# Norms applied on GpSimd to the residual's columns, their statistics spread through DRAM

## The chip, the cores and the metric

The kernel runs on one core of one Trainium2 chip. The metric is the device time of one execution in microseconds (us).

## What is computed

The input is X with 16 x 256 = 4096 tokens of width 128, float32. The block is an FFN, an attention and the FFN again, each added to the residual x:

```python
x = x + 0.5 * ffn(layernorm(x))
x = x + attn(layernorm(x))
x = x + 0.5 * ffn(layernorm(x))
# ffn (hidden width 512, ternary weights w, column scales s; lin(x, w, s) = (x @ w.T) * s)
h = silu(lin(x, w1, s1)) * lin(x, w2, s2)
h = gelu(lin(h, h1, sh1))
h = gelu(lin(h, h2, sh2))
return lin(h, w3, s3)
# attn
h = layer_norm(x) * gamma + beta
keys, values = h @ Wk.T + bk, h @ Wv.T + bv
w = exp((keys @ Wka.T + bka) / sqrt(128))
w = w / cumsum(w, over a sequence of 256)
return cumsum(w * keys) * values
```

## The kernel before

**Tiles.** The 4096 tokens are eight tiles of 512. The residual lies transposed in SBUF as `xt_sb`, with the 128 features on the partitions and the tokens as columns. A second copy of the input, `x_sb`, has tokens on the partitions in blocks of 128. Each tile goes through FFN step t (t = 0 to 7), attention step t (0 to 7), and FFN step t + 8.

**An FFN step.** `p1.m` multiplies the normalised tile with w1 and w2 (m = 0 to 3 are the four blocks of 128 hidden units), ScalarE takes `tanh`, VectorE forms `gate` and `up`. `p2.m`, `gelu2.m` are the second layer, `p3.m`, `gelu3.m` the third, `p4` the last; `dt` adds its result to the residual. TensorE multiplies float32r numbers, so each activation is split: ScalarE's `high` copies it rounded, VectorE's `low` (`act_lo`) subtracts that copy from the full value, and every product is two matmuls. A chunk of p2 or p3 is eight matmuls of 128x128 with 128x512, a chunk of p1 four, p4 eight.

**A norm** (24 of them: 8 for each of the three parts). `stats` is bn_stats on VectorE over blocks with tokens on the partitions. For the first FFN they are blocks of `x_sb`; for attention and the second FFN TensorE first transposes the residual's tile into the PSUM bank `y_ps` (stage `u`, four 128x128 transposes). `aggr` and `veps` on VectorE make mean and variance, `norm` on GpSimd makes `rstd` with a power and `nmr` = -mean x rstd. ScalarE writes the normalised blocks to `z` (`z`, four activations of 128x128), TensorE transposes them into `xt_ps` (stage `t`, four transposes), ScalarE copies that to `xn_hi` and VectorE forms `xn_lo` (FFN), or ScalarE applies gamma and beta and writes `h_t` (attention).

**An attention step.** Three float32 matmuls of `h_t`: `logits` (keys' and logits' weights are folded), `keys`, `values`. ScalarE writes `kw` (exp) and `keys`. VectorE runs `cumsum`, `recip.0`, `recip.1`, `weight` (kw x 1/cumsum), `weight_keys` (x keys), `pool` (cumsum again), `values` and `dt`, which adds to the residual.

**What sets the order.** Every engine works its queue in order; the queues are written out by hand in strings (`START`, `FIRST_STEP`, `ORDER`, `LAST_STEP`), one item per stage and chunk. A step is one FFN tile's second to fourth layer, with the next tile's p1 and the norm after that mixed in (`AHEAD` says how many tiles ahead an item works). The attention items `a:` and `b:` stand in a pattern of three steps that is repeated. Waits are semaphores inside the stages. SyncE's queue loads everything first and then stores the finished tiles. Three flags say whether the weights are exact in float32r; with the given inputs the fast branch runs.

Of the kernel before, what the change touches and what calls it, by code (L numbers as in the profile page):

```python
# [89 lines left out]
LAST_STEP = {  # L90
    "PE": "p2.0 p2.1 p2.2 p2.3 p4 p3.0 p3.1 p3.2 last:p4a last:p3.0 last:p3.1 last:p4b last:p4c.0 last:p4c.1",
    "ACT": "gelu2.0 gelu2.1 high2.0 high2.1 gelu2.2 high2.2 gelu2.3 high2.3 gelu3.0 high3.0 gelu3.1 high3.1 "
           "gelu3.2 high3.2 last:gelu.0 last:gelu.1",
# [905 lines left out]
```

## Time and profile before

| what | value |
| --- | --- |
| median of 3 runs | 377.42 us (376.82 to 377.8) |
| profiled execution, span from first to last instruction | 374.9 us |
| between that span and the median of the runs | 2.5 us |
| PE busy | 368.0 us, 98% |
| DVE (VectorE) busy | 321.9 us, 86% |
| ACT (ScalarE) busy | 314.1 us, 84% |
| POOL (GpSimd) busy | 52.6 us, 14% |

No device time is listed for the profiled execution itself, so its span is set against the median of the other runs. Busy is the time in which an engine has an instruction of its own running; matmuls are pipelined, so their records overlap and their starts, not their durations, tell what one costs.

### The profile page before, as it was taken

Reading aid. Unit: us, or ns where it says so; the run is one execution under the profiler, and the core shown is the slowest. Engines: PE = TensorE matmul, PEld = TensorE weight load, DVE = VectorE, ACT = ScalarE, POOL = GpSimd, SP = SyncE. Lnnn points to the kernel's source line nnn. Section 1 sums busy time; section 2 is a strip of 40 time slices with the busy share of each in tenths; the row PEclk is TensorE's granted clock in tenths of the full one; section 3 lists DMA queues with packets and bytes.
Section 4 is the critical chain, followed back from the end, with each engine's and each line's share of the span. In section 5 each row is a group of like instructions: output and inputs, shape, how many; then the busy total and the mean of one; then the engine's idle time right before and its main releaser. Section 6 shows DMA issues by size and latency. Waiting matters only on the chain.

```text
span 374.9 us, 5278 instructions
## 1 busy us (share of the span) xinstructions
PE 368.0 (98%) x1662; PEld 291.9 (78%) x1662; DVE 321.9 (86%) x713; ACT 314.1 (84%) x549; POOL 52.6 (14%) x67
## 2 busy tenths in 40 slices
PE   7999999999999999999999999999999999999996
PEld 2678888787787877778788787778877778788885
DVE  5898787999999799999988999989799999976733
ACT  4999699989977999798699979967998998686763
POOL 3531101202101202201021120102101210020000
PEclk9999999999999999999999999999999999999999
DMA  7760000000000000000000000000000000000001
GB/s 246 277 265 1 2 0 0 1 2 1 0 2 0 1 2 2 2 0 1 2 0 1 2 1 28 2 28 1 2 29 0 0 30 1 30 1 28 2 0 58
DMA packets 4494, 9.81 MB, mean 26 GB/s; under 512 B 625, under 2 KB 1905, under 8 KB 4209
## 3 DMA queue, kind: packets, MB, share of 16 engines
q1 hardware_dynamic: 3744, 8.65, 6.3%
q10 hardware_dynamic: 720, 0.80, 0.6%
q8 instruction: 15, 0.25, 0.2%
q14 instruction: 15, 0.11, 0.1%
HBM read 7.35 MB, written 2.10 MB: 25 GB/s over the span
## 4 chain that ended last, share of the span: by engine, by line
PE 95%; DMA 2%; DVE 1%; SPq 1%; issue 0%; ACT 0%; ACTq 0%
PE hid_ps L449 60%; PE gate_ps L449 8%; PE y_ps L449 7%; PE up_ps L449 7%; PE xt_ps L462 3%; DMA x_sb<-x 2%; PE y_ps L462 2%; PE xt_ps L632 2%; PE xt_ps L629 2%; PE xt_ps L635 2%; PE up_ps L507 1%; PE gate_ps L507 1%; DVE gate L855 0%; PE xt_ps L449 0%; DVE xt_sb L924 0%
## 5 line engine op out<-in xcount | busy, mean ns | idle before, releaser
L449 PE MATMUL hid_ps<-act_hi,hi_h 128*128 128x512 f32 x480 | 195.6, 408 | 0.0
L449 PE MATMUL hid_ps<-act_lo,hi_h 128*128 128x512 f32 x480 | 186.8, 389 | 0.0
L877 DVE TENSOR_TENSOR act_lo<-full,act_hi 128x512 fp32r<-128x512 f32 x185 | 122.2, 683 | 26.8 <-ACT act_hi L708 24.3
L701 ACT ACTIVATE full<-hid_ps,vec 128x512 f32<-128x512 f32 x123 | 84.4, 686 | 34.9 <-PE hid_ps L449 31.2
L449 PEld LDWEIGHTS hid_ps<-act_hi,hi_h 128*128 128x128 f32 x480 | 90.1, 188 | 22.4 <-issue 4.1
L449 PEld LDWEIGHTS hid_ps<-act_lo,hi_h 128*128 128x128 f32 x480 | 90.2, 188 | 22.1 <-issue 4.3
L708 ACT ACTIVATE act_hi<-full 128x512 fp32r<-128x512 f32 x127 | 78.5, 630 | 2.3
L362 POOL TENSOR_TENSOR rstd<-veps,half 128x4 f32<-128x4 f32 x24 | 35.2, 1467 | 272.5 <-DVE veps L840 272.5
L855 DVE SCALAR_TENSOR_TENSOR gate<-tanh,gate_ps 128x512 f32<-128x512 f32 x60 | 40.6, 679 | 9.2 <-ACT tanh L684 8.6
L684 ACT ACTIVATE tanh<-gate_ps,s_half 128x512 f32<-128x512 f32 x60 | 40.8, 686 | 8.2 <-PE gate_ps L449 8.2
L867 DVE SCALAR_TENSOR_TENSOR full<-up_ps,s_half,gate 128x512 f32<-128x512 f32 x60 | 44.2, 742 | 0.9
L689 ACT ACTIVATE act_hi<-full 128x512 fp32r<-128x512 f32 x60 | 37.3, 621 | 0.2
L940 DVE RECIPROCAL rcsum<-csum 128x256 f32<-128x256 f32 x16 | 27.9, 1743 | 0.0
L449 PE MATMUL gate_ps<-xn_hi,hi_w 128*128 128x512 f32 x59 | 24.7, 419 | 0.0
L726 ACT ACTIVATE z<-y_ps,nmr,rstd 128x128 f32<-128x128 f32 x64 | 24.0, 460 | 0.8 <-POOL nmr L364 0.8
L449 PE MATMUL y_ps<-act_hi,hi_w 128*128 128x512 f32 x60 | 24.2, 403 | 0.0
L449 PE MATMUL y_ps<-act_lo,hi_w 128*128 128x512 f32 x60 | 23.5, 392 | 0.0
L449 PE MATMUL gate_ps<-xn_lo,hi_w 128*128 128x512 f32 x59 | 23.0, 390 | 0.0
L449 PE MATMUL up_ps<-xn_lo,hi_w 128*128 128x512 f32 x59 | 23.0, 390 | 0.0
L449 PE MATMUL up_ps<-xn_hi,hi_w 128*128 128x512 f32 x59 | 23.0, 390 | 0.0
L825 DVE BATCH_NORM_STATS2 stats<-y_ps 128x6 f32<-128x128 f32 x64 | 14.2, 285 | 0.0
L462 PE MATMUL xt_ps<-ident,z 128*128 128x128 f32 x90 | 13.6, 273 | 0.0
(159 smaller groups left out, 397.8 us busy)
## 6 DMA issues: line engine op xcount, KB each, us to landing
xt_sb<-xt SPq DMA_DIRECT2D x1, 2048.0 KB, 10.9
out<-xt_sb SPq DMA_DIRECT2D x7, 256.0 KB, 2.0
x_sb<-x SPq DMA_DIRECT2D x1, 1536.0 KB, 6.6
raw_h<-h2t SPq DMA_DIRECT2D x4, 256.0 KB, 7.3
raw_h<-h1t SPq DMA_DIRECT2D x2, 256.0 KB, 5.9
raw_w<-w2t ACTq DMA_DIRECT2D x1, 256.0 KB, 4.0
raw_w<-w1t SPq DMA_DIRECT2D x1, 256.0 KB, 3.8
raw_h<-h1t ACTq DMA_DIRECT2D x1, 256.0 KB, 6.7
```

The lines of the kernel that those rows point to most:

```text
L362: eng.tensor_tensor(rstd[:, :], veps[:, :], half[:, :], ALU.pow).then_inc(s_pow, 1)
L449: mm = eng.matmul(ps, w, a, start=(first and n == 0), stop=(last and n == len(seq_) - 1))
L462: mm = eng.transpose(dst[:, j * P:(j + 1) * P], src[:, j * P:(j + 1) * P], ident[:, :])
L684: eng.activation(tanh_b[m % 2][:, :], gate_home(T, m)[:, :], ACT.Tanh, scale=s1_half[:, m:m + 1]).then_inc(s_tanh, 1)
L689: eng.activation(act_hi[first_act(T)][:, m, :], full1[m % 2][:, :], ACT.Copy).then_inc(s_hi[1], 1)
L701: eng.activation(full23[m % 2][:, :], home23(n, T, m)[:, :], ACT.Gelu, scale=col("sh1" if n == 2 else "sh2", m)).then_inc(s_gelu[n], 1)
L708: eng.activation(act_hi[n][:, m, :], full23[m % 2][:, :], ACT.Copy).then_inc(s_hi[n], 1)
L726: zz = eng.activation(z[:, j * P:(j + 1) * P], norm_blk(kind, t, j), ACT.Identity, bias=nmr[:, j:j + 1], scale=rstd[:, j:j + 1])
L855: eng.scalar_tensor_tensor(gate_b[m % 2][:, :], tanh_b[m % 2][:, :], 1.0, gate_home(T, m)[:, :], ALU.add, ALU.mult).then_inc(s_gate, 1)
L867: eng.scalar_tensor_tensor(full1[m % 2][:, :], up_home(T, m)[:, :], s12_half[:, m:m + 1], gate_b[m % 2][:, :], ALU.mult, ALU.mult).then_in ...
L877: eng.tensor_tensor(act_lo[a][:, m, :], full[m % 2][:, :], act_hi[a][:, m, :].bitcast(F32), ALU.subtract).then_inc(s_lo[n], 1)
L940: eng.reciprocal(rcsum[:, b], csum[:, b]).then_inc(s_rc, 1)
```

## The change

The first three norms (FFN tiles 0, 1 and 2) stay as they are. The other 21 are made another way:

- VectorE makes only `stats`, now into one of two buffers. `aggregate` on GpSimd combines the two halves of each bn_stats record in seven short operations and takes the power; it leaves -mean and 1/std of all 512 tokens in `pair_b`, 128 partitions x 2 x 4.
- `spread` on SyncE writes these 1024 numbers to a row in DRAM in token order (`rows`), waits until they have landed, and loads the row (4 KB) into every one of the 128 partitions of `wide_b`.
- `xn.0` and `xn.1` on GpSimd add -mean to the residual's tile `xt_tile(t)` and multiply by 1/std, 128x512 each, into `xnt_b`. ScalarE's `t` and VectorE's `t` read `xnt_b` in place of `xt_ps`. The activations to `z` and the transposes `t` are gone.
- The bank `y_ps` is free again after `stats`, not after z.
- In attention `weight` is now kw x keys and `weight_keys` multiplies that by 1/cumsum; the operations are of the same form and number on VectorE.
- The repeated pattern is replaced by sixteen orders for each engine, one per step (`STEPS`), with SyncE's and GpSimd's among them. Items are named by their tile (`a5:stats`, `12:u`); the stores stand among the spreads.

The core of the diff (the other steps' orders, semaphores and the two-buffer bookkeeping are left out). Of the orders, those of steps 7 to 14 of PE, 11 and 12 of ScalarE, and 11 to 13 of VectorE are shown:

```diff
+    "SP": (
...
+        "spread 10:store 11:store store",
+        "store",
+        "store",
+    ),
+    "POOL": (
...
+        "a5:norm a5:xn.0 a5:xn.1 norm 12:norm xn.0 xn.1",
+        "xn.0 xn.1",
+        "a6:norm a6:xn.0 a6:xn.1 norm xn.0 xn.1",
+        "a7:norm a7:xn.0 a7:xn.1 norm xn.0 xn.1",
+        "norm xn.0 xn.1",
...
+        "a3:logits p1.0 p1.1 p2.0 p4 a3:keys u p2.1 p2.2 p2.3 p1.2 a4:u p3.0 p1.3 p3.1 10:u p3.2 p3.3",
+        "a3:values p1.0 p1.1 p2.0 p2.1 p2.2 p2.3 p4 p1.2 p1.3 a4:logits a5:u p3.0 p3.1 a4:keys p3.2",
+        "p1.0 8:p3.3 a4:values p1.1 p4 p2.0 u p2.1 p2.2 p2.3 p1.2 a5:logits 12:u p1.3 p3.0 p3.1 a5:keys p3.2 "
+        "p3.3",
+        "p1.0 p1.1 p2.0 p2.1 p4 p2.2 p2.3 a5:values a6:u p1.2 p1.3 p3.0 p3.1 p3.2 p3.3",
+        "p1.0 p1.1 p2.0 p4 p2.1 u p2.2 p2.3 a7:u p1.2 a6:logits p1.3 p3.0 p3.1 a6:keys p3.2 a6:values p3.3",
+        "p1.0 p1.1 p2.0 p2.1 p4 p2.2 u p2.3 a7:logits p1.2 p1.3 p3.0 p3.1 a7:keys p3.2 a7:values p3.3",
+        "p1.0 p1.1 p2.0 p4 p2.1 u p2.2 p2.3 p1.2 p1.3 p3.0 p3.1 p3.2 p3.3",
+        "p2.0 p2.1 p1.0 p4 p1.1 p2.2 p2.3 p1.2 p1.3 p3.0 p3.1 p3.2 p3.3",
...
+        "tanh.1 gelu2.0 gelu2.1 high2.0 a6:t high2.1 gelu2.2 high2.2 gelu2.3 high1.0 high1.1 tanh.2 high2.3 "
+        "a6:logits tanh.3 gelu3.0 high3.0 a6:keys high1.2 gelu3.1 13:t high1.3 high3.1 gelu3.2 gelu3.3 "
+        "high3.2 high3.3",
+        "gelu2.0 high2.0 tanh.0 tanh.1 gelu2.1 high2.1 gelu2.2 a7:t high2.2 gelu2.3 high1.0 high2.3 tanh.2 "
+        "high1.1 tanh.3 a7:logits high1.2 gelu3.0 a7:keys high3.0 high1.3 gelu3.1 14:t high3.1 gelu3.2 "
+        "high3.2 gelu3.3 high3.3",
...
+        "gate.0 a5:dt dt up.0 stats gate.1 low2.0 up.1 low2.1 low2.2 a7:stats low1.0 gate.2 low2.3 low1.1 "
+        "up.2 a6:cumsum a6:recip.0 gate.3 a6:recip.1 up.3 13:t low3.0 low1.2 low3.1 low1.3 a6:weight "
+        "a6:weight_keys low3.2 a6:pool low3.3",
+        "low2.0 a6:values gate.0 a6:dt dt gate.1 stats low2.1 up.0 low2.2 up.1 low1.0 low2.3 gate.2 up.2 "
+        "gate.3 low1.1 a7:cumsum up.3 low1.2 a7:recip.0 a7:recip.1 low3.0 14:t low3.1 a7:weight low1.3 "
+        "a7:weight_keys low3.2 a7:pool low3.3",
+        "a7:values a7:dt dt gate.0 stats low2.0 low2.1 up.0 gate.1 up.1 low2.2 low1.0 low2.3 low1.1 gate.2 "
+        "up.2 gate.3 low3.0 up.3 low1.2 low3.1 low1.3 low3.2",
...
+BY_PE = (0, 1, 2)
+AGGREGATE = 3
...
+        wide_b = [sb(f"wide_{i}", [P, 2 * TOK]) for i in range(2)]
+        xnt_b = [sb(f"xnt_{i}", [P, TOK]) for i in range(2)]
+        rows = nc.dram_tensor("rows", [2, 2 * TOK], F32).ap()
...
+            def spread(kind, t):
+                i, use = slot(kind, t)
+                eng.wait_ge(s_pow, norm_of[kind, t] + 1)
+                if use > 0:
+                    eng.wait_ge(s_wide[i], 16 * use)
+                eng.dma_start(rows[i].rearrange("(q j p) -> p q j", q=2, j=SUB), pair_b[i][:, :, :],
+                              allow_slow_non_contiguous=True).then_inc(s_parked[i], 16)
+                if use > 0:
+                    eng.wait_ge(s_xn, wide_of[kind, t] - 1)
+                eng.wait_ge(s_parked[i], 16 * (use + 1))
...
+                eng.dma_start(wide_b[i][:, :], rows[i].partition_broadcast(P)).then_inc(s_wide[i], 16)
...
+            def aggregate(n, kind, t):
+                i, use = slot(kind, t)
+                stats, done = stats_b[n % 2], 6 * (n - AGGREGATE)
+                a, b = (1.0 + EPS, EPS * EPS) if n in att_norms else (1.0, EPS)
+                eng.wait_ge(s_bn, SUB * n + SUB)
+                if use > 0:
+                    eng.wait_ge(s_parked[i], 16 * use)
+                eng.tensor_tensor(pair_diff[:, :], stats[:, :, 1], stats[:, :, 4], ALU.subtract).then_inc(s_agg, 1)
+                eng.tensor_tensor(pair_sum[:, :, :], stats[:, :, 1:3], stats[:, :, 4:6], ALU.add).then_inc(s_agg, 1)
+                eng.wait_ge(s_agg, done + 1)
+                eng.tensor_tensor(diff_sq[:, :], pair_diff[:, :], pair_diff[:, :], ALU.mult).then_inc(s_agg, 1)
+                eng.wait_ge(s_agg, done + 2)
+                eng.tensor_scalar(var_part[:, :], pair_sum[:, :, 1], a / P, b, ALU.mult, ALU.add).then_inc(s_agg, 1)
+                eng.wait_ge(s_agg, done + 3)
+                eng.tensor_scalar(diff_part[:, :], diff_sq[:, :], a / 4.0, None, ALU.mult).then_inc(s_agg, 1)
+                eng.tensor_scalar(pair_b[i][:, 0, :], pair_sum[:, :, 0], -0.5, None, ALU.mult).then_inc(s_agg, 1)
+                eng.wait_ge(s_agg, done + 5)
+                eng.tensor_tensor(veps[:, :], var_part[:, :], diff_part[:, :], ALU.add).then_inc(s_ve, 1)
+                eng.wait_ge(s_agg, done + 6)
+                eng.wait_ge(s_ve, n + 1)
+                eng.tensor_tensor(pair_b[i][:, 1, :], veps[:, :], half[:, :], ALU.pow).then_inc(s_pow, 1)
+
+            def xn_add(kind, t):
+                i, use = slot(kind, t)
+                eng.wait_ge(s_wide[i], 16 * (use + 1))
+                if use > 0:
+                    before, at = by_wide[wide_of[kind, t] - 2]
+                    eng.wait_ge(*((s_xlo, at) if before == "ffn" else (s_ht, at + 1)))
+                if kind == "att":
+                    eng.wait_ge(s_x1, t + 1)
+                elif t < NT:
+                    eng.wait_ge(s_xt, 16)
+                else:
+                    eng.wait_ge(s_x2, t - NT + 1)
+                eng.tensor_tensor(xnt_b[i][:, :], xt_tile(t), wide_b[i][:, 0:TOK], ALU.add).then_inc(s_centred, 1)
+
+            def xn_mult(kind, t):
+                i, _ = slot(kind, t)
+                eng.wait_ge(s_centred, wide_of[kind, t] + 1)
+                eng.tensor_tensor(xnt_b[i][:, :], xnt_b[i][:, :], wide_b[i][:, TOK:2 * TOK], ALU.mult).then_inc(s_xn, 1)
...
-            for n in range(2, 3 * NT):
-                norm(n)
...
-                    elif stage == "u" and t >= NT:
+                    elif stage == "u":
                         eng.wait_ge(s_x2, t - NT + 1)
-                        free("y", (s_za, norm_of["ffn", t] + 2))
+                        free("y", (s_bn, SUB * norm_of["ffn", t] + SUB))
                         transpose4(y_ps, xt_tile(t), s_u)
...
+                elif stage == "t" and t not in BY_PE:
+                    i, _ = slot("ffn", t)
+                    eng.wait_ge(s_p1, MC * t)
+                    eng.wait_ge(s_xn, wide_of["ffn", t] + 1)
+                    eng.activation(xn_hi[:, :], xnt_b[i][:, :], ACT.Copy).then_inc(s_xhi, 1)
...
-                    eng.wait_ge(s_t, norm_of["att", t] + 1)
-                    eng.activation(h_t[:, :], xt_ps[:, :], ACT.Identity, bias=col("beta"),
+                    i, _ = slot("att", t)
+                    if t > 0:
+                        eng.wait_ge(s_val, t)
+                    eng.wait_ge(s_xn, wide_of["att", t] + 1)
+                    eng.activation(h_t[:, :], xnt_b[i][:, :], ACT.Identity, bias=col("beta"),
                                    scale=col("gamma")).then_inc(s_ht, 1)
...
+                if n >= AGGREGATE + 2:
+                    eng.wait_ge(s_agg, 6 * (n - 2 - AGGREGATE) + 2)
+                elif n >= 2:
+                    eng.wait_ge(s_nmr, n - 1)
                 for j in range(SUB):
                     if (n, j) == (0, SUB // 2):
                         eng.wait_ge(s_x0_half, 16)
-                    eng.bn_stats(stats[:, j, :], norm_blk(kind, t, j)).then_inc(s_bn, 1)
...
+                    eng.wait_ge(s_keysb, t + 1)
+                    eng.wait_ge(s_wgk, t + 1)
+                    eng.tensor_tensor(wgt[:, :], kw[:, :], keys[:, :], ALU.mult).then_inc(s_wg, 1)
...
-                    eng.tensor_tensor(wgt[:, :], kw[:, :], rcsum[:, :], ALU.mult).then_inc(s_wg, 1)
-                elif stage == "att_weight_keys":
                     eng.wait_ge(s_wg, t + 2)
-                    eng.wait_ge(s_keysb, t + 1)
-                    eng.tensor_tensor(wgt_keys[:, :], wgt[:, :], keys[:, :], ALU.mult).then_inc(s_wgk, 1)
```

## Rows read from the trace of the kernel before

**Rows 1.** The page's busy table: us, share of the span, instructions.

```profile
PE 368.0 (98%) x1662; PEld 291.9 (78%) x1662; DVE 321.9 (86%) x713; ACT 314.1 (84%) x549; POOL 52.6 (14%) x67
```

**Rows 2.** The page's chain that ended last, by engine.

```profile
PE 95%; DMA 2%; DVE 1%; SPq 1%; issue 0%; ACT 0%; ACTq 0%
```

**Rows 3.** Windows; columns as in the first line.

```profile
core 0: us, PE busy (x) PEld busy (x) DVE busy (x) ACT busy (x) POOL busy (x), PEclk, DMA share, GB/s
50.00:350.00 300.00, 300.00 (x1349) 239.75 (x1348) 271.76 (x590) 260.69 (x452) 38.62 (x40) 1.00 0.02 6
200.00:250.00 50.00, 50.00 (x226) 39.70 (x225) 47.65 (x98) 45.22 (x79) 6.26 (x6) 1.00 0.02 6
```

**Rows 4.** Timeline of PE: start, duration, instruction.

```profile
65.12 0.60 PE L462 MATMUL xt_ps<-ident,z 128*128 128x128 f32 x4
65.48 0.48 PE L449 MATMUL y_ps<-act_hi,hi_w 128*128 128x512 f32 x1
65.79 0.40 PE L449 MATMUL y_ps<-act_lo,hi_w 128*128 128x512 f32 x1
```

**Rows 5.** Windows, tile z alone: PE, PEld, DVE, ACT.

```profile
50.00:350.00 300.00, 12.61 (x84) 10.13 (x84) 0.00 (x0) 32.23 (x84) 1.00 0.02 6
```

**Rows 6.** Groups of instructions: count | busy us, mean ns | idle before.

```profile
L362 POOL TENSOR_TENSOR rstd<-veps,half 128x4 f32<-128x4 f32 x24 | 35.2, 1467 | 272.5 <-DVE veps L840 272.5
L364 POOL TENSOR_TENSOR nmr<-neg_mean,rstd 128x4 f32<-128x4 f32 x24 | 8.3, 344 | 1.9
L375 POOL TENSOR_TENSOR act_lo<-full,act_hi 128x512 fp32r<-128x512 f32 x2 | 2.6, 1296 | 2.2 <-ACT act_hi L689 2.2
L764 ACT ACTIVATE xn_hi<-xt_ps 128x512 fp32r<-128x512 f32 x14 | 8.2, 589 | 2.7 <-PE xt_ps L462 2.7
```

**Rows 7.** Windows: tile mv (DVE), then act_lo (PE, PEld, DVE, POOL).

```profile
50.00:350.00 300.00, 12.18 (x120) 1.00 0.02 6
50.00:350.00 300.00, 184.30 (x472) 88.72 (x472) 103.76 (x158) 0.00 (x0) 1.00 0.02 6
```

**Rows 8.** Timeline of POOL and DVE at five places.

```profile
18.29 2.75 POOL L368 CAST hi_h<-raw_h 128x512 fp32r<-128x512 f32 x4
18.45 1.00 DVE L877 TENSOR_TENSOR act_lo<-full,act_hi 128x512 fp32r<-128x512 f32 x1 [0.26 <-POOL act_lo L375]
19.37 0.68 DVE L913 TENSOR_TENSOR xn_lo<-hid_ps,xn_hi 128x512 fp32r<-128x512 f32 x1
...
45.53 1.01 POOL L362 TENSOR_TENSOR rstd<-veps,half 128x4 f32<-128x4 f32 x1 [13.30 <-DVE veps L840]
46.02 0.69 DVE L877 TENSOR_TENSOR act_lo<-full,act_hi 128x512 fp32r<-128x512 f32 x1
...
69.81 0.87 DVE L825 BATCH_NORM_STATS2 stats<-x_sb 128x6 f32<-128x128 f32 x4
...
152.09 2.52 POOL L362 TENSOR_TENSOR rstd<-veps,half 128x4 f32<-128x4 f32 x1 [9.18 <-DVE veps L840]
152.52 0.68 DVE L877 TENSOR_TENSOR act_lo<-full,act_hi 128x512 fp32r<-128x512 f32 x1
153.12 1.27 DVE L951 TENSOR_TENSOR_SCAN pooled<-ones,wgt_keys 128x256 f32<-128x256 f32 x2
```

**Rows 9.** DMA issues: count, KB each, median us from issue to landing.

```profile
out<-xt_sb SPq DMA_DIRECT2D x7, 256.0 KB, 2.0
...
x_sb<-x SPq DMA_DIRECT2D x1, 256.0 KB, 7.1
...
x_sb<-x SPq DMA_DIRECT2D x1, 128.0 KB, 3.0
```

**Rows 10.** The chain in order of time: start, us, what.

```profile
40.79 0.45 PE gate_ps L449 x2
...
43.51 1.81 PE hid_ps L449 x8
...
68.50 0.86 PE xt_ps L632 x2
```

More of the change, by code:

```diff
@@ L64 @@
     ),
     "ACT": (
[10 rows of a table removed]
[41 rows of a table added]
     ),
     "DVE": (
-        "a:stats low2.0 a:aggr t a:veps low2.1 gate.0 up.0 gate.1 up.1 low2.2 gate.2 low1.0 low2.3 dt up.2 low1.1 "
-        "stats gate.3 aggr up.3 veps a:cumsum low3.0 a:recip.0 low1.2 low3.1 low1.3 low3.2 a:recip.1 low3.3",
-        "b:stats a:weight b:aggr t b:veps a:weight_keys low2.0 a:pool gate.0 a:values gate.1 low2.1 a:dt up.0 up.1 "
[6 rows of a table removed]
-    ),
-}
[L90 to L93, printed above, removed]
-    "DVE": "low2.0 low2.1 low2.2 low2.3 low3.0 low3.1 dt low3.2 last:dt.0 last:dt.1",
-}
[40 rows of a table added]
+    ),
+}
@@ L97 @@
 POOL_FIRST = ("norm", 1, 2)
-AHEAD = {"stats": 2, "aggr": 2, "veps": 2, "norm": 2, "zwait": 2, "z": 2, "t": 1, "p1": 1, "tanh": 1, "gate": 1,
-         "up": 1, "high1": 1, "low1": 1, "u": 2, "p4": -1, "dt": -1}
+BY_PE = (0, 1, 2)
+AGGREGATE = 3
+AHEAD = {"stats": 2, "aggr": 2, "veps": 2, "norm": 2, "z": 2, "t": 1, "p1": 1, "tanh": 1, "gate": 1,
+         "up": 1, "high1": 1, "low1": 1, "u": 2, "spread": 2, "xn": 2, "p4": -1, "dt": -1, "store": -1}
 def macaron_block(nc, x, xt, w1t, w2t, h1t, h2t, w3t, wkt, wkat, wvt, wkn, vecs, out, seq):
@@ L111, in macaron_block @@
     assert D == P and TOK % seq == 0
-    GROUP, ATT = 3, 2
-    FIRST = 2
-    LOOPS = NT // ATT
-    assert FIRST + GROUP * LOOPS + 2 == 2 * NT
+    assert all(len(steps) == 2 * NT for steps in STEPS.values())
     with ExitStack() as ctx:
@@ L188, in macaron_block @@
         nmr = sb("nmr", [P, SUB])
+        pair_b = [sb(f"pair_{i}", [P, 2, SUB]) for i in range(2)]
         seen = {("w1", 0): h_t, ("w2", 0): pooled, ("w3", 0): pooled}
@@ L314, in macaron_block, with schedule, step @@
         block = ctx.enter_context(nc.Block())
+        def schedule(engine, emit, part):
+            def step(i, order):
+                for stage, chunk, t in items(order, i):
+                    emit(stage, chunk, t)
+            if part == "start":
+                step(-1 if engine == "PE" else -2, START[engine][0])
+            if part == "first":
+                step(-1, START[engine][1])
+            if part == "second":
+                step(0, SECOND_LAYER)
+            if part == "rest":
+                for i, order in enumerate(STEPS[engine]):
+                    step(i, order)
         @block.sync
@@ L336, in _, with emit @@
             eng.dma_start(xt_sb[:, :], xt).then_inc(s_xt, 16)
-            for t in range(NT - 1):
-                eng.wait_ge(s_x1, NT + t + 1)
-                eng.dma_start(out[:, t * TOK:(t + 1) * TOK], xt_tile(t)).then_inc(s_out, 16)
+            def spread(kind, t):
[9 more added lines that the diff above has]
+                eng.dma_start(wide_b[i][:, :], rows[i].partition_broadcast(P)).then_inc(s_wide[i], 16)
+            def emit(stage, chunk, t):
+                if stage in ("spread", "att_spread"):
+                    spread("ffn" if stage == "spread" else "att", t)
+                elif stage == "store":
+                    eng.wait_ge(s_x1, t + 1)
+                    eng.dma_start(out[:, (t - NT) * TOK:(t - NT + 1) * TOK], xt_tile(t)).then_inc(s_out, 16)
+            schedule("SP", emit, "rest")
             for h in range(2):
@@ L389, in _, with emit @@
             hi("w3", 0)
[L390 to L431 removed]
+            def emit(stage, chunk, t):
+                if stage in ("norm", "att_norm"):
+                    kind = "ffn" if stage == "norm" else "att"
+                    if kind == "ffn" and t in BY_PE:
+                        norm(t)
+                    else:
+                        aggregate(norm_of[kind, t], kind, t)
+                elif stage in ("xn", "att_xn"):
+                    (xn_add, xn_mult)[chunk]("ffn" if stage == "xn" else "att", t)
+            schedule("POOL", emit, "rest")
         @block.tensor
@@ L574, in free, with emit @@
                     last[bank] = [reader]
-                def emit(stage, chunk, t, L):
+                def emit(stage, chunk, t):
                     if stage == "flag":
@@ L596, in emit @@
                             return
[L597 removed]
+                        free("xt", (s_xlo, t))
                         transpose4(xt_ps, z, s_t)
@@ L729, in z_blocks, with emit @@
                     zz.then_inc(s_za, 1)
-            def emit(stage, chunk, t, L):
+            def emit(stage, chunk, t):
                 if stage == "hi":
@@ L881, in batches, with emit @@
                 return [slice(b * seq, (b + 1) * seq) for b in range(TOK // seq)]
-            def emit(stage, chunk, t, L):
+            def emit(stage, chunk, t):
                 if stage == "bits":
@@ L910, in emit @@
                                           ALU.subtract).then_inc(s_xlo_half, 1)
+                elif stage == "t" and t not in BY_PE:
+                    i, _ = slot("ffn", t)
+                    eng.wait_ge(s_xhi, t)
+                    eng.tensor_tensor(xn_lo[:, :], xnt_b[i][:, :], xn_hi[:, :].bitcast(F32),
+                                      ALU.subtract).then_inc(s_xlo, 1)
                 elif stage == "t":
```

164 lines of the change are left out of this document (93 added, 71 removed), and 101 rows, old and new, of tables (FIRST_STEP, ORDER, STEPS).

## The prediction

> **What bounds the kernel now.** I read the page's busy table first [rows 1]: TensorE (PE) is busy 98% of the span, VectorE 86%, ScalarE 84%, GpSimd 14%. A share alone doesn't make a bound, so I read the chain that ended last [rows 2]: 95% of the span is PE, and nearly all of it is matmuls following matmuls. The windows [rows 3] show it by stage: from 50 to 350 us PE is busy in every microsecond at a granted clock of 1.00 (the 2.4 GHz level), with the DMA engines 2% busy. VectorE is busy 271.8 of those 300 us, and from 200 to 250 us 47.7 of 50, where PE still loses nothing. The tail from 350 us, 21.65 of 25 us busy, is not touched.
>
> So time in 50 to 350 us is PE's stream alone. Taking work out of that stream shortens the kernel; taking work off VectorE or ScalarE gives only room. Adding work to VectorE costs nothing until its 28.2 us of room (300 minus 271.8) is used.
>
> **Time against span.** The span is 374.9 us; the median of the runs is 377.42. I take the 2.5 us outside the span as unchanged and count from 377.4. A measurement of this kernel can't tell changes under 0.3% (1.1 us) from none.
>
> **PE: what is removed.** Of 24 norms, 21 no longer transpose their normalised tile z on PE: five of the first FFN, eight of attention, eight of the second FFN. Four such transposes start at 65.12, the next matmul starts at 65.48, and the one after at 65.79 [rows 4]. Matmuls otherwise start 0.227 us apart (eight take 1.81 [rows 10]), so this group costs 0.36, and 0.09 in the stretched next start: 0.45 us. 21 x 0.45 = **9.4 us**. Busy time on the same tile, all 84 transposes, gives 12.6 us [rows 5], but pipelined matmuls overlap in that figure, so it is an upper end. The u transposes of the residual (64 of them) stay, because the statistics still need rows. Logits, keys and values stay, so do all FFN matmuls. Nothing is added to PE.
>
> **ScalarE.** The z activations go: 32.2 us from 50 to 350 us [rows 5], 1.5 us a norm. The copy to xn_hi and the gamma/beta activation stay and read SBUF in place of PSUM. The copy takes 0.59 us now [rows 6], so even at double that from SBUF the 1.5 us removed covers it. Nothing of this shows in the time, since PE never waits for ScalarE now [rows 2]. But ScalarE is in order: its new wait for a finished xnt tile stands in front of gelu and high, so a late tile stops PE through it.
>
> **VectorE.** Aggregation, negated mean and veps go (six short instructions a norm; 20 of the 21 norms lie in the window, one just ahead of it): 12.2 us from 50 to 350 us [rows 7]. Reciprocal, scans, the two products and the residual adds keep their number; weight now multiplies by keys first, same form, 0 us. xn_lo keeps its size but reads two SBUF tiles, which matters only below. PE's stream shrinks to 300 - 9.4 = 290.6 us and VectorE's work to 271.8 - 12.2 = 259.6, so its room is 31 us.
>
> **GpSimd against VectorE: the unknown cost.** 42 new passes of 128x512 with two SBUF inputs run on GpSimd; the only such instructions of before take 1.30 us [rows 6]. 42 x 1.30 = 55 us. Aggregation is seven small operations and a power: at the means of 344 and 1467 ns [rows 6], 3.9 us a norm, 82 us. GpSimd then works some 137 of 290 us: not a bound. What matters is who it blocks. At 18.29 us GpSimd casts of 0.61 us each begin; VectorE's act_lo (two SBUF inputs) at 18.45 takes 1.00 us in place of 0.68, +0.31, while xn_lo with a PSUM input right behind it keeps 0.68 [rows 8]. The other way, the power at 152.09 takes 2.52 us, where it takes 1.01 alone: it ends just after the two scans, which have two SBUF inputs as the act_lo before them has [rows 8]. A small power does not hold VectorE: at 45.53 to 46.54 an act_lo starts beneath it and takes 0.69 [rows 8]. So the eight short ones cost VectorE 0. For the 42 passes, the cast's half gives 0.65 us where a two-input instruction comes next. Such instructions are about half of VectorE's time (act_lo alone is 103.8 of 271.8 us [rows 3, 7], the scans, products and adds come on top), and a pass that comes in a row of them waits itself. Bounds per pass: 0 (it fits beneath gate and up) and 1.30 (VectorE stands for the whole pass). I take 0.45, between the cast's +0.31 and 0.65: 42 x 0.45 = **19 us**. That leaves 12 us of 290 as room, 4%. The window from 200 to 250 us had 4.7% and cost PE nothing [rows 3], so the mean is bearable; passes at a bad moment are not. I allow **2.0 us** of PE stall, a tenth of the 19.
>
> The Trainium skill (SBUF — State Buffer, section "SBUF: two separate sides") says that a VectorE instruction with two SBUF inputs and a GpSimd one that reads SBUF exclude each other for the whole instruction, the loser fully blocked. The cast and the slow power agree; the act_lo beneath the power, undelayed, does not. If every pass met such an instruction at its start, its rule would give the upper bound, 55 us in place of 19; that is the second rival's mechanism.
>
> **The chain through GpSimd, SyncE and DRAM.** A late norm is u on PE, statistics on VectorE, aggregation on GpSimd, a DMA that parks 1024 numbers in DRAM, a DMA that spreads 4 KB to 128 partitions (512 KB), two passes, ScalarE's copy; then p1 may start. SyncE waits between its two DMAs, and a second norm's spread queues behind. Costs from the end of u: statistics 0.87 for the four blocks [rows 8]; aggregation 3.9, and 0.08 between two dependent operations (1.9 us idle over 24 at nmr [rows 6]), 0.5; DMAs: no row shows 4-byte pieces or a broadcast. Landings are 2.0 us for a 256 KB store with idle engines, 3.0 for a 128 KB load in the busy start, 7.1 at worst there [rows 9]. The engines are nearly idle later, so I exclude 7.1 and take 2.5 each (bounds 2.0, 3.0): 5.0. Passes 2.6, copy 0.59, xn_lo some 0.45 beyond the first matmul. Sum **13.9 us**. Lower end: the power at 1.01 [rows 8] and DMAs at 4.0 give 12.4. Upper end: the small operations at double their mean and the power at 2.52 [rows 6, 8], 7.3, DMAs 6.0, passes delayed 0.65 each: 19.6.
>
> The room is what PE has between u and p1.0 of that tile. Eight matmuls take 1.81 us (a chunk of p2, p3 or p4), a chunk of p1 0.91, logits, keys or values 0.86 [rows 10], u as much as the transposes of z, 0.45 [rows 4]. In step 12 (tile 14) five chunks, three attention products and two chunks of p1 follow: 13.5 us. Tile 13 has 15.7, tile 9 16.2, tile 15 16.3, tile 11 16.7; tiles 8, 10 and 12 and the first FFN's have most of a step. So only tile 14 lacks something, 13.9 - 13.5 = 0.4; with some queueing in front of it I write **0.6 us**. Of the attention tiles a6 is among the tightest: after its u come p1.2, p1.3, four chunks of p3, and in the next step p1.0, p1.1, p2.0, p4 and p2.1 before ScalarE reaches its wait, 9.1 + 7.2 = 16.3 us, so nothing more.
>
> **Stores** are moved behind spreads on SyncE. Each waits for a residual that is long done and takes 2.0 us to land, under PE; the last two halves are issued as before. Zero.
>
> **Sum.** 377.4 - 9.4 + 2.0 + 0.6 = **370.6 us** (-1.8%).
>
> **Rivals.**
> 1. *The chain is late.* For: five tiles have under 17 us of room and ScalarE's in-order wait hands a late tile on. Against: the 13.9 us sum. At C us from the end of u, the stalls are the sum of C minus each room. It takes all 9.4 us back at C = 17.5 (4.0 + 1.8 + 1.3 + 1.2 + 0.8 = 9.1). At 18.5: 14.1 us, **382 us**, slower. What decides is 3.6 us more than my sum: aggregation at 7.5 us, or both DMAs at 4.3.
> 2. *VectorE becomes the bound through the shared access.* It fills its room at 31/42 = 0.74 us a pass and cancels the gain at 0.74 + 9.4/42 = 0.96. At 1.1: 377.4 - 9.4 + 42 x 0.36 = **383 us**; at 1.30, 391.5. For: the cast row. Against: passes fit beneath gate, up, statistics and reciprocals.
> 3. *The freed time goes nowhere:* either of these partly, 6 to 10 us of stalls, **376 to 378 us**.
> 4. *No stall at all:* **368.0 us**; I keep it within my forecast.
>
> **Chances.** Forecast (368 to 374) 0.53; chain late 0.18; VectorE bound 0.17; gain mostly eaten 0.12, of which 0.06 is still faster, 0.04 the same, 0.02 slower. Of the two slower rivals 0.02 each ends within the bound. Faster 0.59, same 0.08, slower 0.33. The likeliest case's own range is 367.5 to 374. To hold 8 in 10, the range must reach into both slower rivals: 367.5 to 384; beyond 384 I leave about 0.13, below 367.5 about 0.04 (transposes worth their busy 12.6 us would give 364.8).
>
> **What the profile after would show.** Right: 84 fewer transposes, PE busy throughout 50 to 340 us, act_lo's mean slightly over 683 ns, VectorE's busy share up. Rival 1: PE idle ahead of gate_ps in the late steps, ScalarE waiting at xn_hi for GpSimd. Rival 2: act_lo's maximum near 2 us and PE waiting for act_lo all through, with attention steps worst. My 2.5 us a DMA is wrong if either takes over 4 us from issue to landing. The prediction fails most likely in the lock price or in parking 1024 single numbers.

## The result and the profile after

The changed kernel takes **497.33 us** (median of 4 runs, 496.44 to 498.3) against 377.15 us before (376.82 to 377.8): a ratio of 1.3186, 95% interval 1.3164 to 1.3208. The forecast was 370.6 us and faster. It was wrong in sign and by 127 us. Times from here on are medians of the executions in the chip's usual, faster state; two executions of the kernel with 32-byte pieces and one of that with pairs were in a slower state and are left out.

The busy table of the changed kernel's page answers to [rows 1]; below it is the granted clock in 40 slices of the span, in tenths of full speed:

```profile
PE 396.0 (80%) x1578; PEld 300.8 (61%) x1578; DVE 321.9 (65%) x566; ACT 284.2 (57%) x465; POOL 136.5 (28%) x235
...
PEclk9999997996899969979859797889997978897999
```

The 84 transposes are gone (1662 to 1578 instructions on PE), and ScalarE's work fell by 30 us as expected. But PE is idle for 495.0 - 396.0 = 99.0 us of its span, where it was idle for 6.9 (374.9 - 368.0). And its busy time rose by 28.0 us with 9.4 us of work taken away: it runs at a lower granted clock in places. 92 us of idle time and 28 of busy time make the 120 us by which the spans differ. The chain that ended last answers to [rows 2]:

```profile
DMA 49%; PE 18%; POOL 18%; issue 7%; DVE 6%; ACT 1%; POOLq 0%; SPq 0%; ACTq 0%; DVEq 0%
DMA rows<-pair 36%; DMA wide<-rows 12%; PE hid_ps L626 11%; POOL xnt L558 4%; POOL xnt L563 3%; POOL pair L544 3%; PE y_ps L626 3%; PE gate_ps L626 2%; PE up_ps L626 2%; DVE stats L1017 1%; POOL diff_part L538 1%; DVE act_lo L1069 1%; POOL pair L539 1%; POOL veps L541 1%; POOL pair_diff L531 1%
```

PE was 95% of this chain and is 18%. Half of it is two DMAs, and 36% of the span, 178 us, is one of them: parking a norm's 1024 numbers in DRAM. A landing is the time from a DMA's issue until its data have arrived. The page's list of DMA issues has the medians (count, KB, us), and the trace of `pair_b` the spread of the parking's (min/median/max):

```profile
wide<-rows SPq DMA_DIRECT2D x21, 512.0 KB, 4.0
...
rows<-pair SPq DMA_DIRECT2D x21, 4.0 KB, 10.9
```
```profile
DMA to landing us min/median/max: 8.4/10.9/13.1
```

4 KB take 10.9 us, 512 KB take 4.0. The chain that ended last, in order of time, shows how the norms follow one another (start us, us, what):

```profile
259.86 10.51 DMA rows<-pair
270.44 3.69 DMA wide<-rows
274.19 1.26 POOL xnt L558
275.53 1.26 POOL xnt L563
...
279.59 1.01 POOL pair L544
280.62 10.96 DMA rows<-pair
291.64 4.37 DMA wide<-rows
...
301.01 1.04 POOL pair L544
302.07 10.98 DMA rows<-pair
313.13 3.60 DMA wide<-rows
316.80 1.26 POOL xnt L558
318.15 1.26 POOL xnt L563
319.50 0.64 ACT xn_hi L938
320.27 1.43 PE gate_ps L626 x2
321.70 0.85 PE up_ps L626 x2
```

In this stretch one norm's parking begins some 21 us after the last one's (259.86, 280.62, 302.07), and PE gets its tile at the end. Over the whole run SyncE issues the first parking at 32.9 us and the last at 435.2, 20.1 us apart on the mean and between 9 and 40. Who waited, in total (us, times, longest):

```profile
POOL xnt L558 <- DMA wide<-rows: 238.4, 20, 15.7
ACT xn_hi L938 <- POOL xnt L563: 85.3, 12, 13.7
...
PE hid_ps L626 <- ACT full L879: 43.7, 12, 11.3
...
PE gate_ps L626 <- ACT xn_hi L938: 32.5, 5, 10.4
```

PE waits directly for a late tile (`gate_ps`), and more often through ScalarE's queue: its copy to `xn_hi` stands in front of a gelu (`full`) that PE needs.

Windows around such a wait, as [rows 3] has them:

```profile
50.00:350.00 300.00, 236.13 (x918) 179.69 (x917) 199.70 (x326) 169.96 (x270) 94.40 (x160) 0.88 0.11 27
...
320.00:324.00 4.00, 3.73 (x8) 2.79 (x9) 3.71 (x6) 3.57 (x7) 0.00 (x0) 0.50 0.00 0
324.00:330.00 6.00, 6.00 (x24) 4.82 (x23) 3.55 (x5) 3.02 (x6) 1.51 (x2) 0.84 0.23 89
```

PE was idle for 3.8 us up to 320.27 and then runs at a granted clock of 0.50, the 1.2 GHz level; two matmuls take 0.85 us there in the chain where they take 0.45 in [rows 10]. In the stretch of 50 to 350 us the mean is 0.88 (1.00 before).

PE's timeline shows the same after every long wait. Twelve waits of 3.8 to 11.3 us hold 80 of PE's 99 us of idle time, and behind each of them matmuls are recorded with 0.63 us in place of 0.39. Shorter waits differ: those of 2.4 and 2.5 us (up to 53.39 and 85.15) are followed by matmuls at full clock, that of 1.8 us (up to 109.47) by the lower level from 111.03 on. The first matmuls behind one of the long waits:

```profile
320.27 0.77 PE L626 MATMUL gate_ps<-xn_hi,hi_w 128*128 128x512 f32 x1 [3.82 <-ACT xn_hi L938]
...
321.50 0.63 PE L626 MATMUL up_ps<-xn_hi,hi_w 128*128 128x512 f32 x1
```

### The profile page after: what moved, and what is told of

The parts are those of the page before. It is cut to its first block, busy times and chain, and to the rows that moved or that the text cites. A ratio compares the mean times of both kernels' runs of the same rounds, so it can differ in the third digit from the quotient of the medians.

```text
span 495.0 us, 5157 instructions
## 1 busy us (share of the span) xinstructions
PE 396.0 (80%) x1578; PEld 300.8 (61%) x1578; DVE 321.9 (65%) x566; ACT 284.2 (57%) x465; POOL 136.5 (28%) x235
## 2 busy tenths in 40 slices
DMA packets 29359, 20.93 MB, mean 42 GB/s; under 512 B 22800, under 2 KB 24080, under 8 KB 29072
## 3 DMA queue, kind: packets, MB, share of 16 engines
q1 hardware_dynamic: 28608, 19.75, 13.5%
## 4 chain that ended last, share of the span: by engine, by line
DMA 49%; PE 18%; POOL 18%; issue 7%; DVE 6%; ACT 1%; POOLq 0%; SPq 0%; ACTq 0%; DVEq 0%
DMA rows<-pair 36%; DMA wide<-rows 12%; PE hid_ps L626 11%; POOL xnt L558 4%; POOL xnt L563 3%; POOL pair L544 3%; PE y_ps L626 3%; PE gate_ps L626 2%; PE up_ps L626 2%; DVE stats L1017 1%; POOL diff_part L538 1%; DVE act_lo L1069 1%; POOL pair L539 1%; POOL veps L541 1%; POOL pair_diff L531 1%
## 5 line engine op out<-in xcount | busy, mean ns | idle before, releaser
L626 PE MATMUL hid_ps<-act_hi,hi_h 128*128 128x512 f32 x480 | 201.5, 420 | 45.1 <-ACT full L879 43.7
L626 PE MATMUL hid_ps<-act_lo,hi_h 128*128 128x512 f32 x480 | 195.1, 407 | 1.4 <-DVE act_lo L1069 1.3
L626 PEld LDWEIGHTS hid_ps<-act_hi,hi_h 128*128 128x128 f32 x480 | 95.7, 199 | 76.4 <-ACT full L879 53.4
L558 POOL TENSOR_TENSOR xnt<-xt_sb,wide 128x512 f32<-128x512 f32 x21 | 27.5, 1312 | 238.4 <-DMA wide<-rows 238.4
L938 ACT ACTIVATE xn_hi<-xnt 128x512 fp32r<-128x512 f32 x13 | 8.2, 630 | 85.6 <-POOL xnt L563 85.3
L626 PE MATMUL gate_ps<-xn_hi,hi_w 128*128 128x512 f32 x59 | 30.4, 515 | 32.5 <-ACT xn_hi L938 32.5
L1104 DVE TENSOR_TENSOR xn_lo<-xnt,xn_hi 128x512 fp32r<-128x512 f32 x13 | 9.0, 690 | 66.9 <-ACT xn_hi L938 66.9
L626 PEld LDWEIGHTS gate_ps<-xn_hi,hi_w 128*128 128x128 f32 x59 | 12.9, 218 | 38.7 <-issue 36.6
L563 POOL TENSOR_TENSOR xnt<-xnt,wide 128x512 f32<-128x512 f32 x21 | 27.7, 1317 | 1.6
L953 ACT ACTIVATE h_t<-xnt,vec 128x512 f32<-128x512 f32 x8 | 6.5, 812 | 35.5 <-POOL xnt L563 35.5
## 6 DMA issues: line engine op xcount, KB each, us to landing
rows<-pair SPq DMA_DIRECT2D x21, 4.0 KB, 10.9
```

The lines of the kernel that those rows point to most:

```text
L558: eng.tensor_tensor(xnt_b[i][:, :], xt_tile(t), wide_b[i][:, 0:TOK], ALU.add).then_inc(s_centred, 1)
L563: eng.tensor_tensor(xnt_b[i][:, :], xnt_b[i][:, :], wide_b[i][:, TOK:2 * TOK], ALU.mult).then_inc(s_xn, 1)
L626: mm = eng.matmul(ps, w, a, start=(first and n == 0), stop=(last and n == len(seq_) - 1))
```

## The experiments

Theory 1: the chain through DRAM is late. Theory 2: VectorE is held by the passes (the two operations of 128x512 on GpSimd, `xn.0` and `xn.1`), or the new orders stall by themselves. Every ratio is against the kernel before on the same chip; the chips differ by up to 0.2%, so where two kernels ran on different chips, a small difference is taken from the ratios. The mean length of act_lo (0.683 us before) shows how much VectorE is held.

| kernel | us | ratio, 95% interval | landing of a parking, us | act_lo mean, ns |
| --- | --- | --- | --- | --- |
| changed kernel, 1024 pieces of 4 B | 497.33 | 1.3186 (1.3164 to 1.3208) | 10.9 | 708 |
| no DMAs | 381.72 | 1.0127 (1.0104 to 1.015) | - | 799 |
| 256 pieces of 16 B | 372.31 | 0.9868 (0.9845 to 0.9891) | 2.1 | 746 |
| 128 pieces of 32 B, step of 8 | 382.45 | 1.0134 (1.0109 to 1.0158) | 1.4 | 808 |
| before, with 42 passes | 383.11 | 1.0155 (1.0136 to 1.0173) | - | 792 |
| 256 pieces, passes cut to a column | 368.87 | 0.9797 (0.978 to 0.9813) | 2.1 | 683 |
| no DMAs, passes cut to a column | 368.59 | 0.9783 (0.9767 to 0.9799) | - | 687 |
| 512 pieces of 8 B | 379.19 | 1.006 (1.0039 to 1.0081) | 3.4 | 759 |
| 128 pieces of 32 B, step of 2 | 377.89 | 1.0031 (0.9995 to 1.0067) | 1.4 | 784 |
| GpSimd aggregates ahead, 4 B | 475.17 | 1.2611 (1.2567 to 1.2656) | 11.1 | 712 |
| DMAs not waited for, 4 B | 382.05 | 1.0124 (1.0086 to 1.0162) | 11.4 | 802 |
| GpSimd aggregates ahead, 16 B | 394.07 | 1.0449 (1.0416 to 1.0483) | 2.3 | 759 |
| 256 pieces, passes halved | 373.66 | 0.9905 (0.9889 to 0.9922) | 2.2 | 738 |
| spread issued by GpSimd, 4 B | 491.85 | 1.3055 (1.2996 to 1.3114) | 9.9 | 723 |
| attention norms don't wait, 4 B | 470.34 | 1.2462 (1.2397 to 1.2527) | 10.6 | 728 |

The kernels without DMAs, with passes cut to a column, and with DMAs not waited for leave the 21 norms unapplied, and the last one those of attention. All others compute the whole block.

**No DMAs.** SyncE's spreads are dropped:

```diff
-                eng.wait_ge(s_wide[i], 16 * (use + 1))
+                eng.wait_ge(s_pow, norm_of[kind, t] + 1)
+                eng.wait_ge(s_fill, 4)      # wide_b: constant
```

> The changed kernel without its two DMAs a norm: SyncE only stores, the passes on GpSimd start when the power is done and use a constant tile (0 and 1), so the norms aren't applied. Orders, aggregation and the 42 passes stay. Theory 1 (the time is lost in the chain through DRAM, where parking 1024 single numbers takes 10.9 us and holds SyncE): 368 to 373 us, PE busy throughout, granted clock back at 1.00. Theory 2 (VectorE and GpSimd exclude each other, or the new orders stall by themselves): over 400 us, with PE idle for act_lo or gate.

381.72 us, and the clock is back at 0.999. Its busy table:

```profile
PE 363.4 (96%) x1578; PEld 281.9 (75%) x1578; DVE 336.7 (89%) x566; ACT 284.3 (75%) x465; POOL 155.0 (41%) x239
```

The DMA chain holds 116 of the 120 us, net of what the passes cost at their new moments. But 368 to 373 was missed: something else costs 9 us or more.

**Pieces of 16 bytes.** The transposes of u take every fourth column, and the input's rows are laid out by the same rule for FFN tiles 3 to 7:

```diff
-                eng.dma_start(rows[i].rearrange("(q j p) -> p q j", q=2, j=SUB), pair_b[i][:, :, :],
-                              allow_slow_non_contiguous=True).then_inc(s_parked[i], 16)
+                eng.dma_start(rows[i].rearrange("(q p j) -> p q j", q=2, j=SUB), pair_b[i][:, :, :]).then_inc(s_parked[i], 16)
...
-                        transpose4(y_ps, xt_tile(t), s_u)
+                        transpose_by_four(y_ps, xt_tile(t), s_u)
...
+                    mm = eng.transpose(dst[:, j * P:(j + 1) * P], src.rearrange("a (p j) -> a j p", j=SUB)[:, j, :],
```

> The changed kernel with another order of the tokens on the partitions: the u transposes take every fourth column, so a partition holds four neighbouring tokens, and parking writes 256 pieces of 16 bytes in place of 1024 of 4 bytes; the input's rows are laid out to match. Theory 1: a landing is about 2.1 us plus 9.8 ns a piece (10.9 us at 1024, 2.1 us taken from a store in 128 pieces), so 4.6 us here counting from zero pieces or 3.4 us by the line through both; the chain from the end of u falls from about 23 to 15 us, 369 to 378 us. Theory 2: no change beyond the DMA's own idle time, still over 440 us. If strided columns cost PE more, the u groups show it (0.44 us before).

372.31 us: the whole computation, 1.3% faster than before and 25% faster than the changed kernel. Windows and DMA issues of this kernel:

```profile
50.00:350.00 300.00, 297.94 (x1285) 235.83 (x1284) 278.23 (x448) 236.00 (x375) 129.88 (x193) 1.00 0.14 41
```
```profile
wide<-rows SPq DMA_DIRECT2D x21, 512.0 KB, 3.7
...
rows<-pair SPq DMA_DIRECT2D x21, 4.0 KB, 2.1
```

A parking of the same 4 KB in 256 pieces lands in 2.1 us, and PE is busy 297.9 of 300 us. The spread still moves 11 MB in all and costs nothing that shows.

**Pieces of 32 bytes**, the passes reading with a step of eight numbers (`wide_b` as `"a (p q j) -> a q j p"`):

> The changed kernel with each partition's eight numbers parked as one piece of 32 bytes, 128 pieces in all; the passes on GpSimd read the spread row with a step of 8 numbers. Theory 1: parking lands in 2.1 to 2.5 us, chain 13 to 14 us if a pass still takes 1.3 us: 368 to 375 us. If strided reads lengthen a pass to 2 us, the chain is 15 us and GpSimd holds VectorE longer: 372 to 385. Theory 2: over 440 us.

Landing 1.4 us, but 382.45 us, within the expectation's second branch: the passes take 1893 and 1862 ns on the mean in place of 1394 and 1448, and act_lo 808 ns. The kernel is 10 us slower than with 16-byte pieces though its chain is shorter. The kernel with pairs, below, shows that not all of this is the passes' length.

**The kernel before with 42 passes:**

```diff
                 norm(n)
+                if n > 2:
+                    eng.tensor_tensor(scr_c[:, :], scr_a[:, :], scr_b[:, :], ALU.add).then_inc(s_scr, 1)
+                    eng.wait_ge(s_scr, 2 * n - 2)
+                    eng.tensor_tensor(scr_c[:, :], scr_c[:, :], scr_b[:, :], ALU.mult).then_inc(s_scr, 1)
```

> The kernel before with 42 extra passes of 128x512 on GpSimd (two after each norm from the fourth on, on scratch tiles that nobody reads). Nobody waits for them except the next norm on GpSimd. Theory 1: VectorE's 28 us of room takes what they cost it: within 0.5% of 377.2. My prediction's price of 0.45 us a pass would show as some 19 us more of act_lo, scans and products (act_lo's mean at about 0.78 us). Theory 2: at 0.96 us a pass or more, slower by over 1%.

383.11 us: +5.7 us (1.5%). Theory 1 had said within 0.5% and missed; theory 2 had said over 1%, but for 0.96 us a pass, which is not what is found. The group act_lo (busy us, mean ns) and what the trace says of its durations (min/median/max):

```profile
L886 DVE TENSOR_TENSOR act_lo<-full,act_hi 128x512 fp32r<-128x512 f32 x185 | 142.1, 792 | 19.5 <-ACT act_hi L717 16.9 <-ACT act_hi L698 1.7 <-POOL act_lo L377 0.3
```
```profile
L886 DVE TENSOR_TENSOR act_lo<-full,act_hi x185: 620/684/1780, 14.3 to 375.0; 128x512 fp32r<-128x512 f32 x185
```

The median is 684 ns as ever; a few instructions take up to 1.78 us, one pass longer than they should. VectorE is busy 341.5 us in place of 321.9: 19.6 us over 42 passes, **0.47 us a pass**. The kernel lost 5.7 us by it though VectorE is busy only 89% of the span.

**Passes cut to one column**, with 16-byte pieces and without DMAs (`[:, 0:1]` in both operations; the norms aren't applied):

> The kernel with 16-byte pieces, its passes on GpSimd cut to one column each (so the norms aren't applied); aggregation, both DMAs and all waits stay. If what keeps 372.3 us above the 368.0 of the removed transposes is VectorE held by the passes: 368 to 369.5 us and act_lo's mean back at 0.68 us. If it is the length of the chain or the order: the passes' 2.8 us come off each chain, and otherwise 371 to 372.

> The kernel without DMAs, its passes cut to one column as well. It took 381.7 us with full passes, 9 more than the kernel with 16-byte pieces though its chain is shorter. Theory A (the passes, started right behind the power, hold VectorE where PE is about to need it): 367.5 to 369 us. Theory B (the new orders stall without the DMAs for another reason, a shared buffer or an early tile): 375 us or more.

368.87 and 368.59 us, act_lo back at 683 and 687 ns. On this chip the kernel before takes 376.71, so with short passes the gain is 7.8 and 8.1 us of the 9.4 expected from the removed transposes: the new orders, the aggregation and the DMAs of 16-byte pieces cost at most 1.6 us together. Full passes add 3 us where they start after a DMA (3.4 by the times, 2.7 by the ratios) and 13 us where they start right behind the power. Theory A is right: the same 42 passes cost four to five times as much at other moments. Short passes also take 2.8 us off every chain. Without DMAs the chain is no limit, so the 13 us are VectorE's; with 16-byte pieces the two parts of the 3 us were not separated.

**Pieces of 8 bytes**, two neighbouring tokens on a partition:

> As the kernel with 16-byte pieces, with two neighbouring tokens on a partition: 512 pieces of 8 bytes. A landing is 1.4 us at 128 pieces, 2.1 at 256 and 10.9 at 1024. On a line from 256 to 1024 it is 5.0 us; the chain is 2.9 us longer than with 256 pieces, some 17.5 us, where my first rival had the gain eaten: 375 to 381 us. If the time depends on SyncE's holding as well, more: 385. If the pieces were not what costs, 372.

379.19 us, as expected, but with a landing of 3.4 us, not 5.0: the landing isn't a line from 256 to 1024 pieces. The time is 7 us longer than with 16-byte pieces for 1.3 us more of a landing. The pages' chains that ended last, for pieces of 16 bytes, for pieces of 8, and for the kernel with pairs that comes next:

```profile
PE 76%; DVE 13%; POOL 4%; DMA 3%; issue 2%; ACT 1%; DVEq 0%; POOLq 0%; ACTq 0%; SPq 0%
...
PE 59%; DMA 12%; POOL 12%; DVE 9%; issue 4%; ACT 3%; POOLq 1%; DVEq 0%; ACTq 0%; SPq 0%
...
PE 65%; DVE 23%; issue 6%; ACT 4%; POOL 2%; DVEq 0%; POOLq 0%; ACTq 0%
```

With 8-byte pieces DMAs and GpSimd rise from 7% to 24% of the chain: the norms come late, and there is next to no room for it.

**Pairs side by side**, 128 pieces of 32 bytes:

> As the kernel with 16-byte pieces, with -mean and 1/std of a token side by side, so that a partition parks one piece of 32 bytes (128 in all) and the passes read the spread row with a step of two numbers. Landing 1.4 us in place of 2.1. If a pass keeps its 1.4 us: 370.5 to 372.5 us. If the step of two lengthens it (a step of eight made it 1.9 us): 372.5 to 378.

377.89 us. The passes all but keep their length (1441 and 1465 ns), and the landing is 0.7 us shorter; the kernel is 6 us slower than with 16-byte pieces all the same. The expectation gave 370.5 to 372.5 us for passes of unchanged length, and missed. No DMA is left in the chain that ended last, and VectorE's share rises from 13% to 23%. act_lo's mean is 784 ns in place of 746, so the passes meet VectorE at worse moments; that they do so because they start earlier was not tried by itself. Against the kernel with a step of eight, which has the same landing, this one is 4 us faster: so some 4 of that kernel's 10 us go with its longer passes, and 6 appear without them.

**GpSimd's order.** In steps 3, 9, 11 and 12 both aggregations stand ahead of the passes, for 4-byte and for 16-byte pieces:

```diff
-        "a6:norm a6:xn.0 a6:xn.1 norm xn.0 xn.1",
-        "a7:norm a7:xn.0 a7:xn.1 norm xn.0 xn.1",
+        "a6:norm norm a6:xn.0 a6:xn.1 xn.0 xn.1",
+        "a7:norm norm a7:xn.0 a7:xn.1 xn.0 xn.1",
```

> The changed kernel with 4-byte pieces; only GpSimd's order differs: in the four steps where a tile's aggregation stands behind the passes of the attention tile, both aggregations now stand ahead of them. Theory 1 (the 21 norms form one serial chain of some 20 us each, since GpSimd waits in order for a DMA before it aggregates the next norm and SyncE waits for each parking): each of the four pairs loses the spread (4.0), a pass (1.3) and an aggregation (3.4) from that chain, 8.7 us each, 497 - 35 = 462 us. Theory 2 (each norm is late by its own latency alone, whatever stands behind it): 490 to 500 us.

> The kernel with 16-byte pieces and the same change of GpSimd's order. The serial chain is 12 us a norm there, 252 us of 300, so it isn't what bounds: within 0.5% of 372.3 us (370.5 to 374), either way by where the passes fall on VectorE's work.

475.17 us with 4-byte pieces: 22 us gained, where the serial chain said 35 and single lateness none. 394.07 with 16-byte pieces: a miss by 20 us. In that run ScalarE waits 19.5 us at `h_t` for GpSimd, and GpSimd waits 138 us for statistics where it waited 84: the attention tile's passes stand behind an aggregation that waits for statistics not yet made. The same order gains where the DMA is the later of the two and loses where the statistics are.

**DMAs issued but not waited for**, 4-byte pieces; the passes read a constant tile:

> The changed kernel with both its DMAs a norm issued as they are (1024 pieces of 4 bytes, then the spread), but the passes on GpSimd don't wait for them and read a constant tile (0 and 1; the norms aren't applied). Theory 1 (only the waiting costs): 377 to 386 us, as without DMAs (381.7), and a parking still lands in some 10.9 us. Theory 3 (the many small writes themselves slow the kernel, through memory or DMA queues): over 400 us. If a parking lands much sooner here, its 10.9 us came from something that the waiting kernel does.

382.05 us, the same as without DMAs, and a parking still lands in 11.4 us (8.7 to 13.8). The small writes slow nobody who doesn't wait; waiting for the two DMAs of each norm costs 497.33 - 382.05 = 115 us.

**The last two**, to see how 21 waits become 115 us. First, GpSimd issues the spread, so SyncE never waits for a parking:

```diff
+                eng.wait_ge(s_parked[i], 16 * (use + 1))
+                eng.dma_start(wide_b[i][:, :], rows[i].partition_broadcast(P)).then_inc(s_wide[i], 16)
                 eng.wait_ge(s_wide[i], 16 * (use + 1))
```

> The changed kernel with 4-byte pieces; the spread from DRAM is issued by GpSimd just before its passes, so SyncE issues a parking as soon as the power is done and never waits for one to land. If SyncE's in-order waiting is a share of the 115 us (497 against 382 without waiting): each of the 8 steps with two norms wins some 4 to 9 us, 425 to 465 us. If only GpSimd's own in-order wait counts: 490 to 505 us, a little more where GpSimd's issue takes longer than SyncE's 0.3 us.

491.85 us, 5 us less. This is not all that SyncE's waiting costs: the edit also puts 21 issues of 0.64 us, 13 us in all, and the wait for the parking into GpSimd's queue. It does show that the long waits remain when SyncE's are gone. Second, the eight attention norms don't wait:

> The changed kernel with 4-byte pieces; all DMAs are issued, but the passes of the 8 attention norms don't wait for theirs and read a constant tile (attention's norm isn't applied), so 13 of 21 norms wait. If every norm costs its own lateness: 382 + 13/21 x 115 = 453 us. If what counts is one serial chain through GpSimd of 20 us a waiting norm: 13 x 20.1 + 8 x 6 = 309 us, little over the 300 us at hand, 390 to 405 us.

470.34 us: 27 us less for eight norms, which leaves 88 us with the 13 FFN norms. Both formulas missed (453; 390 to 405). Divided evenly that is 3.4 us for a norm of attention and 6.8 for one of the FFN, but since the norms hold each other up, such shares need not add.

## Why the prediction was wrong

**The step that failed** is in the chain through GpSimd, SyncE and DRAM: "The engines are nearly idle later, so I exclude 7.1 and take 2.5 each (bounds 2.0, 3.0): 5.0." The two landings are 10.9 and 4.0 us, 14.9, where the upper bound was 6.0. The terms beside them held: an aggregation takes 2.6 to 5.0 us in the trace (3.9 and 0.5 forecast), two passes 2.6. My nearest rows were stores and loads of 256 KB and 128 KB in 128 long pieces, and I let bytes and idle engines decide. The number of pieces decided. The text of the change had it: `"(q j p) -> p q j"` writes every number to a place of its own, 21 x 1024 pieces, and the bounds should have had an open top. The page counts them: 22800 packets under 512 bytes, 625 before. The Trainium skill (DMA: Bandwidth & Descriptors, section "Rules for kernel authors") says that a last dimension that isn't contiguous becomes one descriptor per element; the packet count agrees. I knew the count, named it as a likely place to fail, and priced it at nothing.

**Rival 1 had the right mechanism and the wrong size.** It said that both DMAs at 4.3 us would eat the gain, and named five tiles with rooms of 13.5 to 16.7 us. With 14.9 us of DMA in place of 5.0 its C is 23.8 us and its formula gives 5 x 23.8 - 78.4 = 41 us of stalls, 409 us; it is 497. Its signs came: PE idle ahead of `gate_ps`, ScalarE waiting at `xn_hi` for GpSimd, and a DMA over 4 us. Two things were missing. The norms are not late one by one, for which the sum allowed "some queueing" and 0.6 us in all: the parkings follow each other at 20 us on the mean, and part of that is GpSimd, which waits in order for a spread before it aggregates for the next (the changed order alone gave 22 us back). And long idle times cost twice: behind each wait of 3.8 us or more PE runs at the 1.2 GHz level for some us. Compared with the kernel without DMAs, PE has 84 us more idle time (99.0 against 378.1 - 363.4 = 14.7) and 33 us more busy time for the same matmuls. How the 115 us divide between a norm's own lateness and the queues stays open: neither of my two formulas fits both the changed order of GpSimd and the attention norms that don't wait.

**PE: 9.4 us** was right within 1.6 us. With the passes cut short the kernel takes 368.9 and 368.6 us, 7.8 and 8.1 less than the kernel before on that chip.

**ScalarE's own work** was right: 30 us less. **VectorE's** was less of a relief than forecast: its busy time with short passes is 313.8 us, 8.1 less than before, where the window on tile mv gave 12.2. It doesn't change the outcome.

**0.45 us a pass** is the right size but not a constant, and that it meets 0.47 in the kernel before with 42 passes is partly luck. VectorE's busy time above the 313.8 us of short passes, over 42, gives 0.19 us in the changed kernel itself, 0.28 with 16-byte pieces and 0.54 without DMAs. **2.0 us of PE stall** from it was too low: about 3 us with 16-byte pieces, 5.7 in the order of before, 13 without DMAs. The step "a tenth of the 19" had no row behind it. The window that ran at 95% on VectorE without loss misled me. A held act_lo comes late by up to 1.1 us at once, and a mean over 50 us says nothing of that; that this is the whole reason is argued, not shown. The rule of the Trainium skill cited in the prediction (SBUF — State Buffer, "SBUF: two separate sides") holds for the big passes: act_lo's longest grows from 1.00 us to 1.78 with whole passes and to 1.23 with halved ones, as if it waits out one instruction.

**Rivals 2 and 3** did not occur in the changed kernel. Rival 2 asked for 0.96 us a pass to cancel the gain; without DMAs 0.54 us were enough, since PE stalls before VectorE is full. **Stores** cost nothing that an experiment shows.

**A version that beats both** is the kernel with 16-byte pieces, 372.31 us. Halving its passes did not help. The 3 us that it takes above the same kernel with short passes are what VectorE and GpSimd still cost each other, and the 2.8 us by which full passes lengthen each chain.

> The kernel with 16-byte pieces, each pass on GpSimd cut in two of 256 columns (84 of them). If a pass holds VectorE for its whole length and VectorE can go between the halves, a held act_lo waits up to 0.7 us in place of 1.3: the 3.4 us that the passes cost falls to 1 to 2, 370 to 371.5 us. If it is the sum of the passes that counts, 372 to 374, since the fixed part of an instruction is paid twice.

It took 373.66 us: act_lo's mean fell from 746 to 738 ns, but a pass in two parts takes 2 x 0.89 us in place of 1.39. That the longer chain takes back what VectorE gained was not shown apart.

## What to carry to other kernels

Price a DMA by its pieces before its bytes: read the access pattern, count the contiguous runs on the side that is most broken up, and leave the range open at the top if no row of the trace has so many. A permutation that makes each run four numbers long can often be moved to where it is free, here the choice of the columns that a transpose reads. And when a detour saves 9 us on the bounding engine but puts two DMAs and an in-order queue into every norm, compare its length with the room between producer and consumer first: the least room here was 13.5 us, and with 8-byte pieces 1.3 us more of a landing cost 7 us. Shorter is not always better either: with the same work, where the passes fell on VectorE's queue was worth 3 to 13 us, so a new order has to be measured.
